# Counting every fifth group of edge tiles during the message stage of a two-layer graph network on one Trainium2 core

## The chip, the cores and the metric

The kernel runs on one core of one Trainium2 (trn2) chip. The metric is the device time in microseconds (us) of that core, as the median of several executions. The engines are TensorE (PE; its weight loads are shown apart as PEld), VectorE (DVE), ScalarE (ACT), GpSimd (POOL) and SyncE (SP, which here only issues transfers). The engines run their own instruction streams in order and meet at semaphores.

## The reference

There are N = 12,500 nodes with C = 96 features and E = 412,500 directed edges, sorted by target, with 4 features each. Cut to what matters:

```python
h = relu(layernorm(x))                       # nodes
e = mlp(edge_attr)                           # 4 -> 96, relu, batch norm over all edges
m = mlp(concat(h[src], h[dst], e))           # 288 -> 96 per edge, relu, batch norm over all edges
x = x + segment_sum(m, dst) + mlp(h)         # layer 1
h = relu(layernorm(x))
f = segment_sum((h @ W)[src] * dinv[src] * dinv[dst], dst)   # layer 2
x = x + relu(f @ W1 + b1) @ W2 + b2
```

Layer 2's sum over edges acts on 32 columns: W and W1 are multiplied together ahead, so that each node has a row t of 32 numbers, and what is wanted for each target is the sum of t over its sources.

## The kernel before, in words

The edges are cut in 806 blocks of 512 (`ES`), each of 4 tiles of 128. Nodes are padded to 12,800 = 100 columns of 128 (`HI` = 100). The stages run one after the other, with a barrier between them: set-up and node products, a pass over all edges for the statistics of the edge features (which also gathers the rows of every sixth block and keeps them in device memory), **the message stage**, the node stage between the layers, **the counting stage** of layer 2, and the output.

**The message stage** (functions at lines 918 to 1071, streams at 1243 to 1293) is software-pipelined over the 806 blocks. Every engine runs the same `step(k)`, in which some operations belong to block k and others to earlier blocks. What order each engine has in step K:

- PE: `edge_product(K)` (L983, one bf16 product of 512 columns), `message_product(K-1)` (L1017, 4 fp32 products, each shown as 2 loads and 2 products), `sum_edges(K-2)` (L1061, the same).
- DVE: `onehot_T(K)` (L998), `window_rows(K)` (L975), `onehot(K)` (L1005), `add_gathered(K-1)` (L1030), `accumulate(K-2)` (L1052), `add_window(K-2)` (L1071). The first two wait for `message_product(K-2)`, `add_gathered(K-1)` for `message_product(K-1)` and the gathered rows, `add_window(K-2)` for `sum_edges(K-2)`.
- ACT: `copy_indices(K)` (L923), `edge_relu(K-2)` (L990), `message_relu(K-3)` (L1038), `square(K-3)` (L1045).
- POOL: `gather(K)` (L932), 4 indirect transfers of 128 rows each, for 5 of 6 blocks, into one of 4 buffers. It waits until `add_gathered(K-4)` has freed the buffer.
- SP: `load_pair` (L954, L958) loads edge features and target numbers of two blocks, `load_window` (L967) the rows of the window of targets, `load_spilled` (L941) the kept rows.

**The counting stage** (from L1646) takes 3,234 tiles of 128 edges in NG = 154 groups of GT = 21. For tile n, `edge_onehots` (DVE, L1701 and L1702) makes one-hots of 600 and of 128 columns from the source (600 = 100 columns of nodes times 6 slots of targets, `SLOT` = 6), `tile_counts` (PE, L1709) multiplies them in two products of 300 columns, and `keep_counts` (ACT, L1718) copies the 600 counts to `adj` as bf16. There are three buffers between each two of these engines. When a group is complete, `group_sums` (PE, L1731) multiplies its 100 blocks of 128 x 128 counts by t, spread over the last 17 of the next group's 21 tiles; `group_parts`, `group_place` and `group_add` (L1739 to L1753) add the group's targets into the result.

Of the kernel before, what the change touches and what calls it, by code (L numbers as in the profile page):

```python
# [39 lines left out]
QS = GT * SLOT  # L40
NEG = -1e30


class Dims:


    def __init__(self, n, e):
        self.N, self.E = n, e
        self.NCH = -(-(n + W) // CH)
        self.NP = self.NCH * CH  # L50
        self.NT = self.NP // P
        self.SV = -(-e // ES)
        self.S = -(-self.SV // (2 * SPILL)) * 2 * SPILL
        self.EP = self.S * ES
        self.T = self.S * SUP
        self.NG = -(-self.SV * SUP // GT)
        self.TD = GT * self.NG

# [37 lines left out]
def gnn_kernel(nc, d, a, out):  # L96
# [4 lines left out]
    with ctx:  # L101
# [34 lines left out]
        NSPILL = SV // SPILL  # L136
        spilled = dram("spilled", (NSPILL, P, SUP * C))
# [60 lines left out]
        dstbc = x_flat[:, 2 * ES:6 * ES].bitcast(I32).rearrange("p (b s e) -> p b s e", b=2, e=ES)  # L198
# [682 lines left out]
        wraw = x_flat[:, 6 * ES:6 * ES + 2 * C].rearrange("p (b c) -> p b c", b=2)  # L881
# [14 lines left out]
        s_add = signal("s_add", 2)  # L896
        def was_spilled(k):
            return k % SPILL == SPILL - 1
# [44 lines left out]
        def load_pair(sp, i, k):  # L943
            if msgs.absent(i, k):
                return
            if k % HP:
                return
            b = (k // HP) % 2
            e0 = (MT * i + k) * ES
            sp.wait_ge(r_mm.sem, r_mm.at(MT * i + k + 1 - 4))  # L950
            sp.sem_inc(turn, 1)
            for j in range(PARTS):
                r = j * PARTS * KE
                sp.dma_start(rk[r:r + PARTS * KE, b, :, :].rearrange("p s e -> p (s e)"),  # L954
                             attr_rows[:, bass.ds(e0, HP * ES)]).then_inc(r_land[b], 16)
            sp.wait_ge(ohT_ok.sem, ohT_ok.at(MT * i + k + 1 - 4))
            sp.sem_inc(turn, 1)
            sp.dma_start(dstbc[C:P, b, :, :].rearrange("p s e -> p (s e)"),  # L958
                         a["dst_row"][:, bass.ds(e0, HP * ES)].partition_broadcast(W)).then_inc(d_land[b], 16)
# [17 lines left out]
        def edge_product(pe, i, k):  # L977
            if msgs.absent(i, k):
                return
            if k % HP == 0:  # L980
                pe.wait_ge(r_land[(k // HP) % 2], (i * (MT // 4) + k // 4 + 1) * (16 * PARTS))
            pe.wait_ge(r_ok.sem, r_ok.at(MT * i + k - 2))
            pe.matmul(ps_r(k), w36[:, :], rk[:, (k // HP) % 2, k % HP, :], start=True, stop=True).then_inc(r_mm.sem, 1)  # L983
# [8 lines left out]
        def onehot_T(dve, i, k):  # L992
            if msgs.absent(i, k):
                return
            if k % HP == 0:
                dve.wait_ge(d_land[(k // HP) % 2], (i * (MT // 4) + k // 4 + 1) * 16)
            dve.wait_ge(m_mm.sem, m_mm.at(MT * i + k - 2))
            dve.tensor_scalar(lhs[C:P, k % 2, :], dstbc[C:P, (k // HP) % 2, k % HP, :], winid[C:P, bass.ds(MT * i + k, 1)],  # L998
                              None, ALU.is_equal).then_inc(ohT_ok.sem, 1)
# [77 lines left out]


# [163 lines left out]
        with nc.If(windowed):  # L1242
            with nc.Block() as block:
                @block.gpsimd
                def _(g):
                    def step(i, k):
                        gather(g, i, k)
                    msgs.run(g, step, 0)

                @block.sync  # L1250
                def _(sp):
                    def step(i, k):
                        load_pair(sp, i, k)
                        load_window(sp, i, k)
                        load_spilled(sp, i, k)
                    msgs.run(sp, step, 0)

                @block.tensor
                def _(pe):
                    for x in (r_mm, m_mm, s_mm):  # L1260
                        x.start(pe)
                    def step(i, k):
                        edge_product(pe, i, k)
                        message_product(pe, *msgs.earlier(i, k, 1))
                        sum_edges(pe, *msgs.earlier(i, k, 2))
                    msgs.run(pe, step, 2)

                @block.scalar
                def _(act):
                    for x in (r_ok, m_ok, m_sq):  # L1270
                        x.start(act)
                    def step(i, k):
                        copy_indices(act, i, k)
                        edge_relu(act, *msgs.earlier(i, k, 2))
                        message_relu(act, *msgs.earlier(i, k, 3))
                        square(act, *msgs.earlier(i, k, 3))
                    msgs.run(act, step, 3)

                @block.vector
                def _(dve):  # L1280
                    dve.memset(sT[:, 0:NP], 0.0).then_inc(m0, 1)
                    dve.memset(acc[:, :, :], 0.0).then_inc(m0, 1)
                    dve.wait_ge(m0, 2)
                    for x in (ohT_ok, w_ok, m_pre, m_acc, s_add):
# [364 lines left out]
        HI = NT  # L1649
        KW = HI * SLOT  # L1650
        HB = KW // 2
# [15 lines left out]
        o_slot = oh[:, 0:2, :, :].rearrange("p b t w -> p b (t w)")  # L1667
        t_load = sem("t_load")
# [6 lines left out]
        a_zero = sem("a_zero")  # L1675
        e_oh = sem("e_oh")
# [6 lines left out]
        BJ = 4  # L1683
        BPER = [-(-HI * (j + 1) // (GT - BJ)) - -(-HI * j // (GT - BJ)) for j in range(GT - BJ)]

# [4 lines left out]
        def ps_b(g):  # L1690

            return bank[6][:, (g % 2) * P:(g % 2) * P + C]

        def ps_w(g):

            return bank[7][0:H, (g % 2) * P:(g % 2) * P + P]

        def edge_onehots(dve, n):
            if n >= 3:
                dve.wait_ge(a_mm, n - 2)  # L1700
            dve.tensor_scalar(o_key[:, n % 3, :], iota_k, key_f[:, n:n + 1], None, ALU.is_equal)  # L1701
            dve.tensor_scalar(o_lo[:, n % 3, :], iota_l, lo_f[:, n:n + 1], None, ALU.is_equal).then_inc(e_oh, 1)  # L1702
# [10 lines left out]
        def keep_counts(act, n):  # L1713
            g, j = n // GT, n % GT
            act.wait_ge(a_mm, n + 1)
            if j == 0 and g >= 2:
                act.wait_ge(b_mm, g - 1)
            act.activation(adj[:, g % 2, :, j * SLOT:(j + 1) * SLOT].rearrange("p (b h) s -> p b h s", b=2),  # L1718
                           ps_a(n).rearrange("p b (h s) -> p b h s", s=SLOT), ACT.Copy).then_inc(a_ok, 1)

        def group_sums(pe, g, q):

            if q == 0:
                if g == 0:
                    pe.wait_ge(a_zero, 2)
                    pe.wait_ge(t_rest, 2)
                pe.wait_ge(a_ok, GT * (g + 1))
                if g >= 1:
                    pe.wait_ge(b_sum, 2 * g)
            for h in range(sum(BPER[:q]), sum(BPER[:q + 1])):  # L1730
                ins = pe.matmul(ps_b(g), adj[:, g % 2, h, :], t3[:, h, :], start=(h == 0), stop=(h == HI - 1))  # L1731
# [3 lines left out]
        def group_parts(dve, g):  # L1735
            dve.wait_ge(b_mm, g + 1)
            if g >= 2:
                dve.wait_ge(w_mm, g - 1)
            dve.tensor_reduce(part[:, g % 2, :], ps_b(g).rearrange("p (i c) -> p c i", i=PARTS), AX, ALU.add).then_inc(b_sum, 1)  # L1739
            dve.tensor_scalar(o_slot[:, g % 2, :], iota_p[:, :], grel[:, g:g + 1], None, ALU.is_equal).then_inc(b_sum, 1)  # L1740

        def group_place(pe, g):
            pe.wait_ge(b_sum, 2 * g + 2)
            if g >= 1:
                pe.wait_ge(w_add, g)
            pe.matmul(ps_w(g), part[:, g % 2, :], o_slot[:, g % 2, :], start=True, stop=True).then_inc(w_mm, 1)

        def group_add(dve, g):
            base = dve.value_load(gbase_i[:, g:g + 1], min_val=0, max_val=N - 1)
            dve.wait_ge(w_mm, g + 1)  # L1750
            if g >= 1:
                dve.wait_ge(w_add, g)
            nodes_of = sT[0:H, bass.ds(base, P)]  # L1753
            dve.tensor_tensor(nodes_of, nodes_of, ps_w(g), ALU.add).then_inc(w_add, 1)

        with nc.If(windowed):
            with nc.Block() as block:
                @block.sync
                def _(sp):
                    sp.dma_start(t_f.rearrange("p (c k) f -> p c k f", k=CT),  # L1760
                                 t_tab.rearrange("(c p k) f -> p c k f", k=CT, p=P)).then_inc(t_load, 16)
                    sp.wait_ge(t_load, 16)

                @block.gpsimd
                def _(g):
# [3 lines left out]
                    for b in range(2):  # L1769
                        g.memset(adj[:, b, :, QS:P], 0.0).then_inc(a_zero, 1)  # L1770

                @block.tensor
                def _(pe):
# [4 lines left out]
                    for g in range(NG + 2):  # L1778
                        for j in range(GT):
                            if g < NG:  # L1780
                                tile_counts(pe, g * GT + j)
                            if 1 <= g <= NG and j >= BJ:
                                group_sums(pe, g - 1, j - BJ)
                            if g >= 2 and j == 6:
                                group_place(pe, g - 2)

                @block.scalar
                def _(act):
# [4 lines left out]
                    for n in range(TD):  # L1793
# [3 lines left out]
                def _(dve):  # L1797
# [24 lines left out]
                    for g in range(NG + 2):  # L1822
                        for j in range(GT):
                            if g < NG:
                                edge_onehots(dve, g * GT + j)
                            if g >= 2 and j == 2:
                                group_parts(dve, g - 2)
                            if g >= 2 and j == 12:
                                group_add(dve, g - 2)
# [167 lines left out]
```

## Time and profile before

| | |
|---|---|
| time, median of 3 runs | 6530.68 us (6529.23 to 6531.93) |
| time of the profiled execution | 6520.64 us |
| its span, first to last instruction | 6518.9 us |
| mean granted TensorE clock | 0.650 |
| busy: PE, PEld, DVE, ACT, POOL | 5654.6, 4382.9, 4173.9, 3822.2, 3237.0 us |
| message stage, first to last L983 | 922.9 to 4328.8 us |
| counting stage, first to last L1718 | 4627.3 to 6450.6 us |

Busy times are sums over the whole span. Those of the stages differ, so a stage has to be read by its own stretch. A busy PE is not a PE at its peak: the ends of its products are modelled, and the granted clock (0.5 is 1.2 GHz, 1.0 is 2.4 GHz) says how fast it may run.

### The profile page before, as it was taken

The page shows a single profiled execution, that of the slowest core. Times are in us where ns is not written, and L with a number is a line of the kernel's source. Part 1 is how long each engine was busy: PE and PEld are TensorE (multiplying, and loading weights), DVE is VectorE, ACT ScalarE, POOL GpSimd, SP SyncE. Part 2 cuts the span into 40 slices and gives each one's busy share as a digit, 9 for nine tenths or more (in the row PEclk, how much of TensorE's full clock was granted, in tenths as well). Part 3 has the DMA queues.
Part 4 walks back from the last instruction along what each step waited for, and adds up shares of the span by engine and source line. Part 5 has one row for each costly group of instructions (what it writes and reads, how often), then busy time and mean ns, then how long its engine had stood idle before and what let it go on. Part 6 is the DMA issues. An engine that isn't in the chain of part 4 may idle for free. (4 is left out here: it accounts for less than half of the span.)

```text
span 6518.9 us, 128731 instructions
## 1 busy us (share of the span) xinstructions
PE 5654.6 (87%) x38038; PEld 4382.9 (67%) x38038; DVE 4173.9 (64%) x13072; ACT 3822.2 (59%) x7170; POOL 3237.0 (50%) x3406
## 2 busy tenths in 40 slices
PE   6755559999999999999999999977799999999998
PEld 5311127777777777777777777765477777777777
DVE  5577764545454544445454444553799999999996
ACT  3566644434444444444444444433699999999996
POOL 3577757777777777777777777753000000000000
PEclk8555555555555555555555555555799999999998
DMA  4444433333333333333333333321000000000001
GB/s 155 137 123 124 124 83 74 74 76 75 76 75 76 74 76 74 74 76 75 75 75 76 74 75 75 74 79 30 18 2 2 2 2 2 2 2 2 2 2 62
DMA packets 297570, 400.07 MB, mean 61 GB/s; under 512 B 146679, under 2 KB 203015, under 8 KB 296247
## 3 DMA queue, kind: packets, MB, share of 16 engines
q1 hardware_dynamic: 193543, 233.00, 12.1%
q0 software_dynamic: 103344, 158.83, 11.5%
q8 instruction: 323, 5.29, 0.3%
q14 instruction: 360, 2.95, 0.1%
HBM read 333.74 MB, written 57.67 MB: 60 GB/s over the span
## 5 line engine op out<-in xcount | busy, mean ns | idle before, releaser
L932 POOL DMA_INDIRECT gbuf<-a_tab,idxb x2688 | 2580.4, 960 | 859.0 <-issue 812.3
L1718 ACT ACTIVATE nf<-psum 128x600 bf16<-128x600 f32 x3234 | 1824.2, 819 | 4.8 <-PE psum L1709 4.8
L1017 PEld LDWEIGHTS psum<-rhs,lhs 128*128 128x128 f32 x6448 | 1434.3, 327 | 365.8 <-issue 365.8
L1017 PE MATMUL psum<-rhs,lhs 128*128 128x96 f32 x6448 | 1628.7, 434 | 13.5 <-DVE rhs L975 13.5
L1038 ACT ACTIVATE msg<-pre 128x384 f32<-128x384 f32 x806 | 421.8, 523 | 1991.2 <-DVE pre L1030 1988.7
L1030 DVE TENSOR_TENSOR pre<-psum,gbuf 128x384 f32<-128x384 f32 x806 | 448.2, 556 | 1613.6 <-issue 1130.0
L1709 PE MATMUL psum<-x_all 128*128 128x300 bf16 x6468 | 1358.8, 291 | 121.6 <-DVE x_all L1702 44.6
L1061 PE MATMUL psum<-oh,msg 128*97 128x32 f32 x6448 | 1171.1, 344 | 282.4 <-ACT msg L1038 276.7
L1061 PEld LDWEIGHTS psum<-oh,msg 128*97 128x97 f32 x6448 | 1134.0, 282 | 364.1 <-ACT msg L1038 358.7
L1701 DVE TENSOR_SCALAR x_all<-x_all,dstrel 128x600 bf16<-128x600 f16 x3234 | 1193.8, 369 | 87.4 <-PE psum L1709 63.0
L1731 PE MATMUL psum<-x_all,nf 128*128 128x96 bf16 x15400 | 1074.4, 205 | 1.0 <-ACT nf L1718 1.0
L1731 PEld LDWEIGHTS psum<-x_all,nf 128*128 128x128 bf16 x15400 | 937.7, 97 | 165.9 <-issue 1.8
L1702 DVE TENSOR_SCALAR x_all<-x_all,src_i 128x128 bf16<-128x128 bf16 x3234 | 788.2, 244 | 0.0
L1709 PEld LDWEIGHTS psum<-x_all 128*128 128x128 bf16 x6468 | 421.5, 96 | 360.8 <-DVE x_all L1702 241.8
L793 PE MATMUL psum<-x_all,w 36*96 36x512 bf16 x806 | 394.4, 638 | 280.7 <-DMA x_all<-attr_parts 278.1
L836 DVE BATCH_NORM_STATS2 sT<-x_all 96x6 f32<-96x512 f32 x806 | 493.1, 676 | 181.0 <-ACT x_all L813 180.5
L744 POOL DMA_INDIRECT gbuf<-a_tab,idxb x536 | 506.0, 944 | 179.3 <-issue 150.6
L813 ACT ACTIVATE x_all<-psum,par 96x1024 f32<-96x1024 f32 x403 | 425.5, 1105 | 231.7 <-PE psum L793 229.1
L990 ACT ACTIVATE lhs<-psum,par 96x512 f32<-96x512 f32 x806 | 539.2, 669 | 3.9
L983 PE MATMUL psum<-x_all,w 36*96 36x512 bf16 x806 | 530.9, 659 | 4.5 <-DMA x_all<-attr_parts 4.4
L793 PEld LDWEIGHTS psum<-x_all,w 36*96 36x96 bf16 x806 | 118.0, 180 | 556.5 <-DMA x_all<-attr_parts 490.3
L1052 DVE TENSOR_TENSOR acc<-acc,sq 128x384 f32<-128x384 f32 x806 | 441.9, 548 | 0.6 <-ACT sq L1045 0.6
(198 smaller groups left out, 3340.3 us busy)
## 6 DMA issues: line engine op xcount, KB each, us to landing
gbuf<-a_tab,idxb POOLq DMA_INDIRECT x3224
x_all<-dst_row SPq DMA_DIRECT2D x403, 128.0 KB
x_all<-attr_parts SPq DMA_DIRECT2D x807, 36.0 KB
x_all<-attr_parts SPq DMA_DIRECT2D x1209, 24.0 KB
spilled<-gbuf SPq DMA_DIRECT2D x134, 192.0 KB, 1.9
gbuf<-spilled SPq DMA_DIRECT2D x134, 192.0 KB
x_all<-b_tab SPq DMA_DIRECT2D x806, 12.0 KB
attr_parts<-sT SPq DMA_DIRECT2D x72, 136.0 KB, 1.9
```

What stands on the lines that cost most here:

```text
L744: g.indirect_dma_start(gbuf[:, j, t, :], None, a_tab[:, :], bass.IndirectOffsetOnAxis(ap=idxb[:, j, t:t + 1], axis=0)).then_inc(x_land[j], 16)
L793: pe.matmul(bank[k % 6][0:C, :], w36[:, :], ek[:, q % NB, k % HG, :], start=True, stop=True).then_inc(e_mm.sem, 1)
L932: g.indirect_dma_start(gbuf[:, k % 4, t, :], None, a_tab[:, :], bass.IndirectOffsetOnAxis(ap=idxb[:, k % 4, t:t + 1], axis=0)).then_inc(g_ ...
L983: pe.matmul(ps_r(k), w36[:, :], rk[:, (k // HP) % 2, k % HP, :], start=True, stop=True).then_inc(r_mm.sem, 1)
L990: act.activation(lhs[0:C, k % 2, :], ps_r(k), ACT.Relu, bias=par[:, B_EDGE:B_EDGE + 1]).then_inc(r_ok.sem, 1)
L1017: ins = pe.matmul(ps_m(k)[:, t, :], lhs[:, k % 2, t * TILE:(t + 1) * TILE], rhs[:, k % 2, :], start=True, stop=True)
L1061: ins = pe.matmul(ps_s(k), msg[:, k % 2, t, :], oh[:, k % 4, t, :], start=(t == 0), stop=(t == SUP - 1))
L1701: dve.tensor_scalar(o_key[:, n % 3, :], iota_k, key_f[:, n:n + 1], None, ALU.is_equal)
L1702: dve.tensor_scalar(o_lo[:, n % 3, :], iota_l, lo_f[:, n:n + 1], None, ALU.is_equal).then_inc(e_oh, 1)
L1709: ins = pe.matmul(ps_a(n)[:, b, :], o_lo[:, n % 3, :], o_key[:, n % 3, b * HB:(b + 1) * HB], start=True, stop=True)
L1718: act.activation(adj[:, g % 2, :, j * SLOT:(j + 1) * SLOT].rearrange("p (b h) s -> p b h s", b=2), ps_a(n).rearrange("p b (h s) -> p b h s ...
L1731: ins = pe.matmul(ps_b(g), adj[:, g % 2, h, :], t3[:, h, :], start=(h == 0), stop=(h == HI - 1))
```

## The change

Of the 154 groups, 30 (numbers 4, 9, 14, ... 149) are taken out of the counting stage and counted in the message stage, one tile in each of 21 of 26 steps; the last 26 of the 806 steps have none. So 630 steps get a tile and 176 don't.

- Message stage, DVE: after `window_rows(K)` and ahead of `onehot(K)`, `early_keys` (in one of 26 steps: six small operations on 21 columns, each waiting for the one before) and `early_onehots(K)` (the one-hots of 600 and 128 columns).
- PE: `early_counts(K, 0)` between `edge_product(K)` and `message_product(K-1)`, and `early_counts(K, 1)` between that and `sum_edges(K-2)`: a bf16 product of 300 columns each. The first waits for this step's one-hots.
- ACT: after `edge_relu(K-2)`, two `early_keep` (128 x 300, to bf16), each waiting for its product, and at a group's end two transfers to device memory (`adj_tab`), each 128 x 6,300 bf16 = 1.61 MB.
- SP: the edge features of a pair of blocks come in one transfer and not in three; the target numbers come block by block, in two buffers of one block (two of two before).
- A few operations ahead of the message stage's steps (iota, two copies, two products with 315 columns, two subtractions).
- Counting stage: 124 groups of 21 tiles go through it as before; `group_sums` of a group is spread over the last 14 tiles (`BJ` = 7). The counts of the 30 early groups are loaded from device memory in four pieces, 3.23 MB a group, as soon as the products of the early group before are done, and `early_sums` multiplies their 100 blocks, spread over the 42 tiles of the windows w with w % 4 of 2 and 3.

```diff
+        self.early = [g for g in range(4, self.NG, 5)][:self.SV // EARLY]
...
-            for j in range(PARTS):
-                r = j * PARTS * KE
-                sp.dma_start(rk[r:r + PARTS * KE, b, :, :].rearrange("p s e -> p (s e)"),
-                             attr_rows[:, bass.ds(e0, HP * ES)]).then_inc(r_land[b], 16)
-            sp.wait_ge(ohT_ok.sem, ohT_ok.at(MT * i + k + 1 - 4))
+            sp.dma_start(rk[:, b, :, :].rearrange("p s e -> p (s e)"),
+                         attr_rows[:, e0:e0 + HP * ES].unsqueeze(0).to_broadcast([PARTS, PARTS * KE, HP * ES])
+                         ).then_inc(r_land[b], 16)
+
+        def load_targets(sp, i, k):
+            sp.wait_ge(ohT_ok.sem, ohT_ok.at(MT * i + k - 2))
             sp.sem_inc(turn, 1)
+            sp.dma_start(dstbc[C:P, k % 2, :],
+                         a["dst_row"][:, bass.ds((MT * i + k) * ES, ES)].partition_broadcast(W)).then_inc(d_land[k % 2], 16)
...
+        def early_tile(k):
+            g, j = k // EARLY, k % EARLY
+            return (g, j, g * GT + j) if g < NE and j < GT else None
+
+        def early_onehots(dve, k):
...
+            if n >= 2:
+                dve.wait_ge(n_mm, 2 * (n - 1))
+            dve.tensor_scalar(key_e[:, n % 2, :], iota_ke, keys[:, e % 2, j:j + 1], None, ALU.is_equal)
+            dve.tensor_scalar(low_e[:, n % 2, :], iota_le, lows[:, e % 2, j:j + 1], None, ALU.is_equal).then_inc(n_oh, 1)
+
+        def early_counts(pe, k, b):
...
+            if b == 0:
+                pe.wait_ge(n_oh, n + 1)
+            if n:
+                pe.wait_ge(n_ok, 2 * n + b - 1)
+            pe.matmul(bank[6 + b][:, 0:HB], low_e[:, n % 2, :], key_e[:, n % 2, b * HB:(b + 1) * HB],
+                      start=True, stop=True).then_inc(n_mm, 1)
+
+        def early_keep(act, k, b):
...
+            act.wait_ge(n_mm, 2 * n + b + 1)
+            if j == 0 and b == 0 and e:
+                act.wait_ge(o_adj, 32 * e)
+            act.activation(stage[:, b * HI // 2:(b + 1) * HI // 2, j * SLOT:(j + 1) * SLOT],
+                           bank[6 + b][:, 0:HB].rearrange("p (h s) -> p h s", s=SLOT), ACT.Copy).then_inc(n_ok, 1)
+
+        def early_store(act, k):
...
+            act.wait_ge(n_ok, 2 * GT * (e + 1))
+            for b in range(2):
+                act.dma_start(adj_tab[e, :, b * HI // 2 * QS:(b + 1) * HI // 2 * QS],
+                              stage[:, b * HI // 2:(b + 1) * HI // 2, :].rearrange("p h s -> p (h s)")).then_inc(o_adj, 16)
...
                     def step(i, k):
                         edge_product(pe, i, k)
+                        early_counts(pe, MT * i + k, 0)
                         message_product(pe, *msgs.earlier(i, k, 1))
+                        early_counts(pe, MT * i + k, 1)
                         sum_edges(pe, *msgs.earlier(i, k, 2))
...
                         copy_indices(act, i, k)
                         edge_relu(act, *msgs.earlier(i, k, 2))
+                        early_keep(act, MT * i + k - 2, 0)
+                        early_keep(act, MT * i + k - 2, 1)
+                        early_store(act, MT * i + k - 2)
                         message_relu(act, *msgs.earlier(i, k, 3))
...
                         onehot_T(dve, i, k)
                         window_rows(dve, i, k)
+                        early_keys(dve, MT * i + k)
+                        early_onehots(dve, MT * i + k)
                         onehot(dve, i, k)
...
-        BJ = 4
+        BJ = 7
...
+        def early_load(sp, e):
+            if e == 0:
+                sp.wait_ge(t_rest, 2)
+            else:
+                sp.wait_ge(h_mm, e)
...
-                    for g in range(NG + 2):
+                    for w in range(ND + 2):
                         for j in range(GT):
-                            if g < NG:
-                                tile_counts(pe, g * GT + j)
-                            if 1 <= g <= NG and j >= BJ:
-                                group_sums(pe, g - 1, j - BJ)
-                            if g >= 2 and j == 6:
-                                group_place(pe, g - 2)
+                            if w < ND:
+                                tile_counts(pe, w * GT + j)
+                            if w >= 2 and j == 3:
+                                group_place(pe, w - 2, False)
+                            if 1 <= w <= ND and j >= BJ:
+                                group_sums(pe, w - 1, j - BJ)
+                            if w % 4 >= 2 and w // 4 < NE:
+                                early_sums(pe, w // 4, (w % 4 - 2) * GT + j)
+                            if w % 4 == 0 and 1 <= w // 4 <= NE and j == 10:
+                                group_place(pe, w // 4 - 1, True)
...
-                    for n in range(TD):
+                    for n in range(ND * GT):
                         keep_counts(act, n)
```

## Rows read from the trace of the kernel before

**Rows 1.** The page: tenths busy in 40 slices of the span.

```profile
PE   6755559999999999999999999977799999999998
ACT  3566644434444444444444444433699999999996
POOL 3577757777777777777777777753000000000000
PEclk8555555555555555555555555555799999999998
```

**Rows 2.** Windows: length, then busy us of PE, PEld, DVE, ACT, POOL; clock, DMA.

```profile
1120.00:4300.00 3180.00, 2921.05 (x12829) 2467.63 (x12828) 1580.26 (x4524) 1294.61 (x2890) 2413.74 (x2515) 0.50 0.31 75
5000.00:5100.00 100.00, 95.38 (x1233) 73.31 (x1230) 92.99 (x381) 100.00 (x179) 0.00 (x0) 1.00 0.01 2
```

**Rows 3.** The page, costliest groups: POOL's gathers and ACT's copies of counts.

```profile
L932 POOL DMA_INDIRECT gbuf<-a_tab,idxb x2688 | 2580.4, 960 | 859.0 <-issue 812.3
L1718 ACT ACTIVATE nf<-psum 128x600 bf16<-128x600 f32 x3234 | 1824.2, 819 | 4.8 <-PE psum L1709 4.8
```

**Rows 4.** Line 983, once a step: its duration in ns, first and last start in us.

```profile
L983 PE MATMUL psum<-x_all,w x806: 631/659/660, 922.9 to 4328.8; 36*96 36x512 bf16 x162
```

**Rows 5.** Timeline of the weight loads, 2000 to 2013 us: start, length, line.

```profile
2004.12 0.15 PEld L983 LDWEIGHTS psum<-x_all,w 36*96 36x96 bf16 x1
2004.71 1.78 PEld L1017 LDWEIGHTS psum<-rhs,lhs 128*128 128x128 f32 x8 [0.44 <-issue]
2006.37 1.43 PEld L1061 LDWEIGHTS psum<-oh,msg 128*97 128x97 f32 x8
2007.86 0.15 PEld L983 LDWEIGHTS psum<-x_all,w 36*96 36x96 bf16 x1
...
2011.60 0.15 PEld L983 LDWEIGHTS psum<-x_all,w 36*96 36x96 bf16 x1
```

**Rows 6.** Timeline of VectorE in the same stretch.

```profile
2003.06 0.56 DVE L1030 TENSOR_TENSOR pre<-psum,gbuf 128x384 f32<-128x384 f32 x1 [1.11 <-PE psum L1017]
2003.54 0.55 DVE L1052 TENSOR_TENSOR acc<-acc,sq 128x384 f32<-128x384 f32 x1
2004.33 0.19 DVE L1071 TENSOR_TENSOR sT<-sT,psum 97x32 f32 x1 [0.24 <-PE psum L1061]
2004.55 0.60 DVE L998 TENSOR_SCALAR lhs<-x_all,winid 32x512 f32<-32x512 int32 x1
2005.07 0.24 DVE L975 TENSOR_TENSOR rhs<-x_all,cstb 32x96 f32<-32x96 f32 x1
2005.34 0.29 DVE L1005 TENSOR_TENSOR oh<-iota_p,dstrel 128x128 f32<-128x128 f32 x1
...
2008.91 0.49 DVE L998 TENSOR_SCALAR lhs<-x_all,winid 32x512 f32<-32x512 int32 x1
2009.33 0.25 DVE L975 TENSOR_TENSOR rhs<-x_all,cstb 32x96 f32<-32x96 f32 x1
```

**Rows 7.** Timeline of VectorE, counting stage: the one-hots of two tiles.

```profile
6202.94 0.37 DVE L1701 TENSOR_SCALAR x_all<-x_all,dstrel 128x600 bf16<-128x600 f16 x1
6203.22 0.25 DVE L1702 TENSOR_SCALAR x_all<-x_all,src_i 128x128 bf16<-128x128 bf16 x1
6203.39 0.37 DVE L1701 TENSOR_SCALAR x_all<-x_all,dstrel 128x600 bf16<-128x600 f16 x1
```

**Rows 8.** Timeline of PE, counting stage: counts and sums, two tiles.

```profile
5000.48 0.42 PE L1709 MATMUL psum<-x_all 128*128 128x300 bf16 x2
5000.74 0.37 PE L1731 MATMUL psum<-x_all,nf 128*128 128x96 bf16 x5
5001.00 0.43 PE L1709 MATMUL psum<-x_all 128*128 128x300 bf16 x2
```

**Rows 9.** Timeline of VectorE, set-up: small operations that wait for each other.

```profile
9.79 0.25 DVE L364 TENSOR_TENSOR cstb<-trep,acc 4x96 f32<-4x96 f32 x1
10.07 0.20 DVE L365 CAST acc<-cstb 4x96 bf16<-4x96 f32 x1
```

**Rows 10.** Windows at the output's loads (columns as in Rows 2), and the issue of x.

```profile
6460.00:6470.00 10.00, 7.75 (x32) 7.30 (x31) 1.89 (x8) 2.67 (x5) 0.00 (x0) 0.50 0.97 398
...
L265 SPq DMA_DIRECT2D x_all<-x x2: 419/4108/7797, 3.2 to 11.0; - x2
```

More of the change, by code:

```diff
@@ L40 @@
 QS = GT * SLOT
+EARLY = 26
 NEG = -1e30
@@ L57, in __init__ @@
         self.TD = GT * self.NG
+        self.early = [g for g in range(4, self.NG, 5)][:self.SV // EARLY]
+        self.late = [g for g in range(self.NG) if g not in self.early]
+        self.NE, self.ND = len(self.early), len(self.late)
 class Signal:
@@ L1719, in keep_counts, with group_sums @@
                            ps_a(n).rearrange("p b (h s) -> p b h s", s=SLOT), ACT.Copy).then_inc(a_ok, 1)
-        def group_sums(pe, g, q):
+        def group_sums(pe, w, q):
             if q == 0:
-                if g == 0:
+                if w == 0:
                     pe.wait_ge(a_zero, 2)
                     pe.wait_ge(t_rest, 2)
[L1727 to L1731, printed above, removed]
+                pe.wait_ge(a_ok, GT * (w + 1))
+                if w >= 1:
+                    pe.wait_ge(w_add, w)
+            for h in share(HI, GT - BJ, q):
+                ins = pe.matmul(bank[6][:, 0:C], adj[:, w % 2, h, :], t3[:, h, :], start=(h == 0), stop=(h == HI - 1))
@@ L1732, in group_sums @@
             if q == GT - BJ - 1:
                 ins.then_inc(b_mm, 1)
[L1735 to L1746, printed above, removed]
@@ new lines, in early_sums, with sums_of @@
+        def early_sums(pe, e, q):
+            if q == 0:
+                if e == 0:
+                    pe.wait_ge(h_zero, 4)
+                pe.wait_ge(h_land, 64 * (e + 1))
+                if e >= 1:
+                    pe.wait_ge(hw_add, e)
+            for h in share(HI, 2 * GT, q):
+                ins = pe.matmul(bank[7][:, 0:C], early_block(h), t3[:, h, :], start=(h == 0), stop=(h == HI - 1))
+            if q == 2 * GT - 1:
+                ins.then_inc(h_mm, 1)
+        def sums_of(early):
+            return (bank[7], 1, h_mm, h_sum, hw_mm, hw_add, d.early) if early else (bank[6], 0, b_mm, b_sum, w_mm, w_add, d.late)
@@ new lines, in group_parts, with group_place @@
+        def group_parts(dve, n, early):
+            ps, k, mm, summed, placed, added, groups = sums_of(early)
+            g = groups[n]
+            dve.wait_ge(mm, n + 1)
+            dve.tensor_reduce(part[:, k, :], ps[:, 0:C].rearrange("p (i c) -> p c i", i=PARTS), AX, ALU.add).then_inc(summed, 1)
+            dve.tensor_scalar(o_slot[:, k, :], iota_p[:, :], grel[:, g:g + 1], None, ALU.is_equal).then_inc(summed, 1)
+        def group_place(pe, n, early):
+            ps, k, mm, summed, placed, added, groups = sums_of(early)
+            pe.wait_ge(summed, 2 * n + 2)
+            pe.matmul(ps[0:H, P:2 * P], part[:, k, :], o_slot[:, k, :], start=True, stop=True).then_inc(placed, 1)
@@ L1762, in _ @@
                     sp.wait_ge(t_load, 16)
+                    for e in range(NE):
+                        early_load(sp, e)
                 @block.gpsimd
```

181 lines of the change are left out of this document (147 added, 34 removed).

## The prediction

> **What bounds the kernel now.** I read the slices of the page first, then windows by stage, then the costliest groups, then timelines of single steps. The slices show two long regimes [rows 1]. In the message stage PE is busy nine tenths at a granted clock of 0.5 (1.2 GHz), POOL seven tenths, ACT four. In the counting stage ACT is full, PE nearly, the clock is 1.0 (2.4 GHz) and POOL is idle.
>
> Counting stage: ACT is busy 100 of 100 us [rows 2], 3,234 copies in 1,824.2 us [rows 3], so 0.564 us a tile.
>
> Message stage: the 806 steps start from 922.9 to 4328.8 us [rows 4], 4.23 us a step. PE at its fastest needs 3.74: L983 starts at 2004.12 and 2007.86, and again 3.74 later at 2011.60 [rows 5]. The rest is POOL's: 2,688 gathers cost 2580.4 busy and 812.3 idle "issue" us [rows 3], 1.26 us each; 4 gathers in 5 of 6 steps make 4.21 us a step. So the stage runs at POOL's pace, with 0.49 us a step of slack on PE.
>
> **The step with a tile.** The sum of added work isn't what counts here; the order is. Write K for a step with a tile. DVE ends its step K-1 with `add_window(K-3)`, which waits for `sum_edges(K-3)`, the last thing in PE's step K-1. Only then come `onehot_T(K)`, `window_rows(K)` and the new one-hots. PE, after `edge_product(K)`, now waits for those one-hots ahead of `message_product(K-1)`; before, that product needed only DVE's step K-1. So PE and DVE take turns: a ring from the end of PE's step through half of DVE's and back, once a step. Along it, from the start of L983(K):
>
> - `add_window` starts at +0.21 (2004.12 to 2004.33), L998 at +0.43 [rows 5, 6]. L975 follows L998 by 0.42 in one step and 0.52 in the other, L1005 follows L975 by 0.27 [rows 6]. In L1005's place stands the new one-hot, at +1.12 to +1.22.
> - The second one-hot starts 0.28 later and takes 0.25 [rows 7]: ready at +1.65 to +1.75. I take 1.70.
> - `early_counts(K, 0)`: no row has this product at 1.2 GHz. L983 is the nearest: 0.15 load, then 0.44 until the next load starts, 0.59 for 512 columns [rows 5]. 512 columns at 1.2 GHz are 0.43, 300 are 0.25; with the load 0.40. Bounds 0.25 (load hidden) and 0.41. Then `message_product` starts at +2.10 where it started at +0.59: **+1.51**.
> - `early_counts(K, 1)`: again 0.40, bounds 0.25 and 0.41 (L983 behind L1061 pays the load in full [rows 5]).
>
> Together 3.74 + 1.51 + 0.40 = **5.65 us** a step with a tile, with the lower ends 5.30, with the upper 5.72. The new waits for ACT are off this ring: `early_keep` stands behind `edge_relu`, and ACT is idle over half the stage [rows 2]. Queued behind `early_keep(K, 1)` is `message_relu(K-1)`, which needs DVE's addition behind `message_product(K-1)` and so could hardly start earlier. POOL, at 4.21, is now ahead of everybody: its four buffers are full when a step without a tile comes.
>
> **The message stage.** 630 steps at 5.65 are 3,560. The 150 steps without a tile between groups run from full buffers at PE's 3.74: 561. The last 26 stay at 4.23: 110. `early_keys`: 6 linked operations at 0.28 [rows 9], 1.7 us in the ring, 30 times: 50. The lead-in: 3. Sum 4,284 before transfers.
>
> The stores: 3.23 MB a group onto queues that carried 75 GB/s at a share of 0.31 [rows 2]. At 398 GB/s [rows 10] a group is 8 us of all engines, in the 5 steps without a tile, when loads and gathers have least slack. ACT may also be held at its second issue (a second large one took SP 7.8 us, the first 0.42 [rows 10]); 2 to 3 us of that pass unseen, since the message it delays is multiplied a step later. Bounds 0 and 10 us a group; I take 1.5, since buffers are full then: 45. SP's load of target numbers is issued two steps ahead, 7.5 us at the least, and it has two transfers less to issue per pair: nothing; without that cover it would be a wait in the ring.
>
> Stage: 4,329. Before: 806 x 4.23 = 3,409. **+920** (with the ends of the step, +700 to +960; with those of the stores, -45 and +255 more).
>
> **The counting stage.** 630 copies less: 630 x 0.564 = **-355**. PE per tile: two counts and five or six sums take 0.52 [rows 8]; the two counts 0.26 (5000.48 to 5000.74), and the 5.9 sums of a tile (100 over 17) the other 0.26, 0.044 each. In the 60 windows that also carry early sums, a window's PE work is 21 x 0.26 + 150 x 0.044 = 12.1 and some 0.3 for placing; ACT's is 21 x 0.564 = 11.8. In its last 14 tiles PE needs 0.26 + 9.5 x 0.044 = 0.68 a tile, in the first 7 0.36, and three buffers carry only two tiles across. So 0.5 us a window is lost: **+30** (bounds 0 and 100). DVE's one-hots run at 0.45 a tile alone [rows 7], below 0.564. The early loads have two windows, 23.7 us, for 3.23 MB: 136 GB/s against 398 seen [rows 10], hidden; without that cover each would hold PE, 30 times.
>
> **Sum.** 920 - 355 + 30 = +595. The profiled execution took 6520.6, the median of the runs 6530.7, 10 us above. So 6520.6 + 595 = 7116 on its scale and 7,125 as a median.
>
> **A rule against one term.** The row: behind L983 the next load starts only after 0.44 us of idle PEld, when the product's columns have gone through [rows 5], so I charged loads in full. The Trainium skill (TensorE: Matmul & The Clock Gate, Part 2: What happens when you issue a matmul) says that PE pulls the next weight load ahead of running products, into a background buffer. By that rule both early products would cost their columns alone. What this would make is the second rival below.
>
> **The rivals.**
>
> 1. The ring doesn't close: the one-hots arrive in time, and only PE's work counts. Then 26 steps cost PE 21 x 4.54 + 5 x 3.74 = 114 us against POOL's 110: +4 in 30 rounds, 120; with 50 and 45 for keys and stores and -325 for counting, 6,420. With products at 0.25, 6,300. For it: DVE is busy only half the stage [rows 2]. Against: the chain `sum_edges`, `add_window`, one-hots, product is in program order on both engines, and in rows 6 the wait of L1071 for PE shows. This is the case in which the change is faster. Chance 0.07.
> 2. The ring closes with hidden loads: 630 x 0.30 = 189 less, 6,935. Chance 0.12.
> 3. Stores disturb the stage: the steps without a tile wait out 8 to 10 us a group, or ACT's held issue delays sums by several us: +240 more, 7,370. Chance 0.10.
> 4. PE takes over as the bound of the whole counting stage, or waits for early loads: 5 us a window lost in the 60 is +300; a third of that is likelier, 7,220. Chance 0.08.
> 5. The clock rises to 2.4 GHz in the message stage, since bf16 products are added. For it: the counting stage, with such products, has 1.0 [rows 2]. Against: it is 0.50 over the whole stretch [rows 2], steps in which PE never pauses [rows 5] among them, and in the ring PE stands still a fifth of the time. PE's part of the ring would halve, the ring would fall to 3.7 and POOL bind again: -325 and some 95, 6,300. Chance 0.03.
>
> **How the numbers follow.** The forecast, steps of about 5.65 us and the counting stage down by 325, has 0.60. The range runs from the second rival to the third: with the ends of the terms 6,890 to 7,400. Faster by over 0.2% (about what a measurement of this kernel can tell from no change) are rivals 1 and 5, 0.10; within 0.2% only an accident of both, 0.01; slower 0.89.
>
> **What the changed profile would show.** L983 first to last some 900 us further apart; steps of 5.6 to 5.7 us in runs of 21, then five of 3.7; before the early product PE idle over 1 us, ended by the second early one-hot on DVE; POOL idle for `add_gathered`. The clock 0.5. The counting stage with 2,604 copies in about 1,500 us, ACT full but for two windows in four. I'm wrong if steps with a tile take 4.6 us or less, or if PE's wait ahead of the early product is absent.

## The result: 6907.9 us against 6530.8, 5.8% slower

The changed kernel took 6907.89 us (6905.49 to 6908.81), the kernel before 6530.79 (6529.23 to 6531.93); the ratio is 1.0577 (95% interval 1.0559 to 1.0595). Forecast were 7,125 us and a range of 6,890 to 7,400. The profiled execution took 6907.84 us, its span is 6905.1.

The page of the changed kernel, tenths busy in 40 slices, and the groups that answer to [rows 1, 3]:

```profile
PE   7655558888888888888888888888967999999998
ACT  3566634444444444444444444444424999999996
...
POOL 3677756666666666666666666666631000000000
PEclk7555555555555555555555555555556999999998
...
L970 POOL DMA_INDIRECT gbuf<-a_tab,idxb x2688 | 2587.1, 962 | 1506.8 <-issue 896.5
L1861 ACT ACTIVATE nf<-psum 128x600 bf16<-128x600 f32 x2604 | 1521.9, 760 | 11.2 <-PE psum L1852 4.8
...
L1164 PEld LDWEIGHTS psum<-x_all 128*128 128x128 bf16 x1260 | 194.3, 154 | 1058.7 <-DVE x_all L1153 1058.7
```

In the message stage TensorE went from nine tenths to eight and GpSimd from seven to six, though there is more to do, and no engine is fuller than TensorE's eight: the sign of a wait, not of a new full engine. GpSimd's idle time before its gathers went from 859 to 1507 us, so it no longer sets the pace. The last line names the wait: 1058.7 us of idle weight loading ahead of the early product (L1164), ended by the second early one-hot (L1153). The clock stayed at 0.5.

The stage's length is read from L1024, the edge product (L983 before), that of the counting stage from L1861 (L1718 before), the first and the last start:

```profile
L1024 PEld LDWEIGHTS psum<-x_all,w x806: 148/152/153, 937.3 to 5010.5; 36*96 36x96 bf16 x162
...
L1861 ACT ACTIVATE nf<-psum x2604: 652/716/1092, 5309.3 to 6836.5; 128x600 bf16<-128x600 f32 x186
```

Message stage: 4073.2 us, against 4328.8 - 922.9 = 3405.9 [rows 4]: +667. Counting stage: 1527.2 us against 1823.3: -296. The rest of the span's +386 is the start: L983 ran twice ahead of a 10.7 us clearing before; L1024 first runs behind it, 14 us later.

One counted step of the changed kernel, weight loads and then VectorE (start, length), which answers to [rows 5, 6]:

```profile
3003.80 0.15 PEld L1024 LDWEIGHTS psum<-x_all,w 36*96 36x96 bf16 x1
3005.62 0.10 PEld L1164 LDWEIGHTS psum<-x_all 128*128 128x128 bf16 x1 [1.66 <-DVE x_all L1153]
3005.80 1.78 PEld L1057 LDWEIGHTS psum<-rhs,lhs 128*128 128x128 f32 x8
3007.40 0.20 PEld L1164 LDWEIGHTS psum<-x_all 128*128 128x128 bf16 x1
3007.62 1.52 PEld L1101 LDWEIGHTS psum<-oh,msg 128*97 128x97 f32 x8
3009.20 0.15 PEld L1024 LDWEIGHTS psum<-x_all,w 36*96 36x96 bf16 x1
```

```profile
3004.01 0.19 DVE L1111 TENSOR_TENSOR sT<-sT,psum 97x32 f32 x1 [0.52 <-PE psum L1101]
3004.23 0.60 DVE L1038 TENSOR_SCALAR lhs<-x_all,winid 32x512 f32<-32x512 int32 x1
3004.75 0.24 DVE L1016 TENSOR_TENSOR rhs<-x_all,cstb 32x96 f32<-32x96 f32 x1
3005.03 0.38 DVE L1152 TENSOR_SCALAR x_all<-x_all,rstd 128x600 bf16<-128x600 f16 x1
3005.32 0.25 DVE L1153 TENSOR_SCALAR x_all<-x_all,mean 128x128 bf16<-128x128 bf16 x1
```

The ring can be read off by going back and forth: TensorE's last product ends, VectorE adds the window (4.01), makes the message's one-hot and window rows, the early one-hots (5.03, 5.32), and TensorE's early load starts at 5.62, 0.05 us after the second has ended. Between its edge product and that load the loader stands idle 1.66 us; 0.44 us of this stood there before the change as well [rows 5]. The step takes 9.20 - 3.80 = 5.40 us. Most steps take 5.29 or 5.39, by whether L1038 takes 0.48 or 0.60: 5.34 in the mean.

### The profile page after: what moved, and what is told of

The parts are those of the page before. It is cut to its first block and busy times, and to the rows that moved or that the text cites. A ratio compares the mean times of both kernels' runs of the same rounds, so it can differ in the third digit from the quotient of the medians.

```text
span 6905.1 us, 129865 instructions
## 1 busy us (share of the span) xinstructions
PE 5617.6 (81%) x38042; PEld 4418.8 (64%) x38042; DVE 4287.1 (62%) x13256; ACT 4072.6 (59%) x7800; POOL 3245.4 (47%) x3411
## 5 line engine op out<-in xcount | busy, mean ns | idle before, releaser
L1057 PE MATMUL psum<-rhs,lhs 128*128 128x96 f32 x6448 | 1600.5, 430 | 0.0
L1861 ACT ACTIVATE nf<-psum 128x600 bf16<-128x600 f32 x2604 | 1521.9, 760 | 11.2 <-PE psum L1852 4.8
L1057 PEld LDWEIGHTS psum<-rhs,lhs 128*128 128x128 f32 x6448 | 1435.1, 327 | 126.2 <-issue 78.0
L1175 ACT ACTIVATE x_all<-psum 128x300 bf16<-128x300 f32 x1260 | 534.0, 424 | 1586.3 <-PE psum L1164 1586.2
L1101 PEld LDWEIGHTS psum<-oh,msg 128*97 128x97 f32 x6448 | 1206.3, 285 | 14.8 <-ACT msg L1078 8.9
L1164 PE MATMUL psum<-x_all 128*128 128x300 bf16 x1260 | 561.2, 446 | 740.9 <-DVE x_all L1153 740.9
L1101 PE MATMUL psum<-oh,msg 128*97 128x32 f32 x6448 | 1132.0, 338 | 7.6 <-ACT msg L1078 7.6
L1852 PE MATMUL psum<-x_all 128*128 128x300 bf16 x5208 | 1071.6, 291 | 76.2 <-DVE x_all L1845 30.6
L1844 DVE TENSOR_SCALAR x_all<-x_all,dstrel 128x600 bf16<-128x600 f16 x2604 | 966.6, 371 | 101.0 <-PE psum L1852 11.0
L1164 PEld LDWEIGHTS psum<-x_all 128*128 128x128 bf16 x1260 | 194.3, 154 | 1058.7 <-DVE x_all L1153 1058.7
L1874 PE MATMUL psum<-x_all,nf 128*128 128x96 bf16 x12400 | 804.8, 205 | 0.6 <-DVE sT L1934 0.6
L1874 PEld LDWEIGHTS psum<-x_all,nf 128*128 128x128 bf16 x12400 | 715.3, 97 | 108.6 <-ACT nf L1861 0.8
L1845 DVE TENSOR_SCALAR x_all<-x_all,src_i 128x128 bf16<-128x128 bf16 x2604 | 640.0, 246 | 0.0
L1024 PE MATMUL psum<-x_all,w 36*96 36x512 bf16 x806 | 531.1, 659 | 16.6 <-DVE x_all L1417 12.6
```

The costliest lines, as they stand in the source:

```text
L1057: ins = pe.matmul(ps_m(k)[:, t, :], lhs[:, k % 2, t * TILE:(t + 1) * TILE], rhs[:, k % 2, :], start=True, stop=True)
L1101: ins = pe.matmul(ps_s(k), msg[:, k % 2, t, :], oh[:, k % 4, t, :], start=(t == 0), stop=(t == SUP - 1))
L1164: pe.matmul(bank[6 + b][:, 0:HB], low_e[:, n % 2, :], key_e[:, n % 2, b * HB:(b + 1) * HB], start=True, stop=True).then_inc(n_mm, 1)
L1175: act.activation(stage[:, b * HI // 2:(b + 1) * HI // 2, j * SLOT:(j + 1) * SLOT], bank[6 + b][:, 0:HB].rearrange("p (h s) -> p h s", s=SL ...
L1844: dve.tensor_scalar(o_key[:, n % 3, :], iota_k, key_f[:, col:col + 1], None, ALU.is_equal)
L1845: dve.tensor_scalar(o_lo[:, n % 3, :], iota_l, lo_f[:, col:col + 1], None, ALU.is_equal).then_inc(e_oh, 1)
```

## The experiments

The theory: the message stage grew because `early_counts(K, 0)` waits for one-hots that VectorE can't begin before TensorE has ended its step before. The rivals: it is the added work wherever it stands; it is the stores. A second question came from the trace: why the early products cost 0.43 us a step where the forecast had 0.80.

Experiments e1 to e4 ran on a chip on which the kernel before itself took 7747.96 us (7735.55 to 7770.36). It has no trace of its own there. The nearest is that of e4, which is the kernel before but for wider weights: its counting stage was as long as ever (1824.2 us), its message stage took 4426.5 us instead of 3406, and its engines stood for times that the profile puts down to no one ("issue", "remote"). So those four tell by ratios and by steps without a pause, and e1 to e3 were run again, on chips with the usual time. e1, e5, e6, e11 and e12 were timed 4 to 10 times; e2 to e4 and e7 to e10 once, so they tell by their traces and by differences well above the spread of one kernel's runs (6518 to 6529 us in 13 runs of the kernel before, beside e9).

**e1 and e5: the early tiles one step later.** All the work is kept; TensorE multiplies in step K the one-hots that VectorE made in step K-1.

```diff
-                        early_counts(pe, MT * i + k, 0)
+                        early_counts(pe, MT * i + k - 1, 0)
                         message_product(pe, *msgs.earlier(i, k, 1))
-                        early_counts(pe, MT * i + k, 1)
+                        early_counts(pe, MT * i + k - 1, 1)
...
-                        early_keep(act, MT * i + k - 2, 0)
-                        early_keep(act, MT * i + k - 2, 1)
-                        early_store(act, MT * i + k - 2)
+                        early_keep(act, MT * i + k - 3, 0)
+                        early_keep(act, MT * i + k - 3, 1)
+                        early_store(act, MT * i + k - 3)
```

> TensorE and ScalarE take each early tile one step later (early_counts of block K-1 in step K, early_keep likewise), with all the work kept. Ring theory (TensorE waits in every counted step for one-hots that VectorE can only start once TensorE's step before has ended): the wait of about 1.0 us is gone, a counted step costs TensorE 3.74 + 0.43 = 4.17 us, below GpSimd's 4.21 a step, so the message stage falls from 4073 to about 3430 us and the time from 6908 to about 6270 us, faster than the kernel before. Rival, it is the added work: the order of the steps changes nothing, 6908 us. Rival, the stores to device memory: their part stays, some 6300 to 6400 us, with the waits in the five steps without a tile.

Measured: 7594.64 us, 0.9791 (0.9760 to 0.9822) of the kernel before. The sign turned, against the kernel before on the same chip; a step without a pause took 4.05 us.

> The same kernel as e1_later (early tiles taken one step later by TensorE and ScalarE), beside a kernel before that takes its usual 6530 us. On the first chip steps without a pause took TensorE 4.05 us instead of 5.3, below GpSimd's 4.21 a step. Ring theory: about 6270 us. If it is the added work whatever the order: 6908 us. If the stores hold the five steps without a tile: 6300 to 6400 us.

Measured: 6246.27 us (6244.77 to 6250.02) against 6522.91, ratio 0.9578 (0.9564 to 0.9593). The trace of e5: weight loads of one step, then, for the stretch from 1120 to 4300 us, the longest waits of GpSimd and of the addition of the gathered rows (total us, times, longest).

```profile
3000.79 0.15 PEld L1024 LDWEIGHTS psum<-x_all,w 36*96 36x96 bf16 x1
3001.38 0.11 PEld L1164 LDWEIGHTS psum<-x_all 128*128 128x128 bf16 x1 [0.44 <-issue]
3001.38 1.84 PEld L1057 LDWEIGHTS psum<-rhs,lhs 128*128 128x128 f32 x8
3003.05 0.20 PEld L1164 LDWEIGHTS psum<-x_all 128*128 128x128 bf16 x1
3003.26 1.52 PEld L1101 LDWEIGHTS psum<-oh,msg 128*97 128x97 f32 x8
3004.84 0.15 PEld L1024 LDWEIGHTS psum<-x_all,w 36*96 36x96 bf16 x1
```

```profile
DVE pre L1070 <- issue: 772.5, 308, 8.1
POOL gbuf L970 <- issue: 759.5, 2491, 0.3
```

Of the idle 1.66 us the 0.44 behind L1024 are left, and the step is 4.05 us. The stage's first and last L1024 start at 935.0 and 4349.2: 3414 us, 8 more than before the change, with all 630 tiles in it. GpSimd sets the pace again, back to back with 0.3 us between gathers; the additions wait up to 8.1 us. (The profile names no releaser for them; that it is the gathered rows is read from the program's order.) The added work costs TensorE 4.05 - 3.74 = 0.31 us in such a step, which stays under GpSimd's 4.21. So neither the added work (it is all there) nor the stores made the +667: the order did.

**e2 and e9: the early one-hots first in VectorE's step; e3 and e10: behind `onehot(K)`.** If a ring exists, its length follows the place of its members. (With the early one-hots go the early keys.)

```diff
+                        early_keys(dve, MT * i + k)
+                        early_onehots(dve, MT * i + k)
                         onehot_T(dve, i, k)
                         window_rows(dve, i, k)
-                        early_keys(dve, MT * i + k)
-                        early_onehots(dve, MT * i + k)
                         onehot(dve, i, k)
```

> On VectorE the early one-hots stand first in the step, ahead of onehot_T and window_rows, with the same work. Ring theory: the ring is shorter by these two, 0.41 + 0.41 us or a little less, so a counted step falls from 5.3 to 5.4 us to about 4.6 us, the time from 6908 to about 6440 us. Rival, it is the added work: no change, 6908 us.

> On VectorE the early one-hots stand behind onehot(K), with the same work. Ring theory: the ring is longer by that operation, 0.28 us, so a counted step takes about 5.6 us and the time is 6908 + 630 x 0.28 = about 7085 us. Rival, it is the added work: no change, 6908 us.

On the first chip, one run each: 7887.37 and 8002.80 us; steps without a pause of 4.48 and 5.49 us, where the changed kernel has 5.34.

> The same kernel as e2_first (early one-hots first in VectorE's step), beside a kernel before that takes its usual 6520 to 6530 us. On the first chip the counted step without a pause fell from 5.34 to 4.48 us. Ring theory: 630 x 0.86 = 540 us less than the changed kernel, about 6370 us; TensorE's step is then 0.3 us above GpSimd's 4.21. Rival, added work: 6908 us.

> The same kernel as e3_last (early one-hots behind onehot), beside a kernel before that takes its usual 6520 to 6530 us. On the first chip the counted step rose from 5.34 to 5.49 us. Ring theory: 630 x 0.15 = 95 us more, about 7000 us. Rival, added work: 6908 us.

Measured, one run each: 6417.53 us with the one-hots first, 7018.60 with them last; the changed kernel lies between at 6908. One step of e9 in its weight loads, one of e10:

```profile
3002.50 0.15 PEld L1024 LDWEIGHTS psum<-x_all,w 36*96 36x96 bf16 x1
3003.58 0.10 PEld L1164 LDWEIGHTS psum<-x_all 128*128 128x128 bf16 x1 [0.93 <-DVE x_all L1153]
...
3007.16 0.15 PEld L1024 LDWEIGHTS psum<-x_all,w 36*96 36x96 bf16 x1
```

```profile
3000.49 0.15 PEld L1024 LDWEIGHTS psum<-x_all,w 36*96 36x96 bf16 x1
3002.41 0.11 PEld L1164 LDWEIGHTS psum<-x_all 128*128 128x128 bf16 x1 [1.76 <-DVE x_all L1153]
...
3005.98 0.15 PEld L1024 LDWEIGHTS psum<-x_all,w 36*96 36x96 bf16 x1
```

Same instructions, three orders. The rows of e9 and of the changed kernel show the longer of their two common steps, that of e10 the shorter; by the median over the 630 early loads TensorE's wait ahead of them is 0.75, 1.57 and 1.76 us. e9 is 490 us faster, of 540 expected: its steps are 4.48 or 4.66 us. e10 adds 111 us, of 95 expected; from the place alone e3 had expected 0.28 us a step and found 0.15 in the first run and 0.19 in the mean here (5.53 against 5.34), part of it because L1038 is in its slow form of about 0.60 us in 42 of 600 steps instead of 227.

**e12: the early keys off the ring.** The six small operations move to the last of the five steps without a tile (those of the first group stay in step 0).

```diff
-            if k >= SV or k % EARLY or k // EARLY >= NE:
+            if k and (k % EARLY != EARLY - 1 or (k + 1) // EARLY >= NE):
                 return
-            e = k // EARLY
+            e = (k + 1) // EARLY
```

> The changed kernel with early_keys one step earlier, in the last of the five steps without a tile, so that its six operations are off the ring. Ring theory: the first counted step of each group falls from 6.8 us to 5.3 to 5.4, 30 x 1.45 = 43 us, to about 6865 us. Rival, the same work stays on VectorE, no change: 6908 us.

Measured: 6865.24 us (6862.09 to 6866.54), 43 us less than the changed kernel; the first counted step of a group takes 5.38 us instead of 6.80. The same operations at the same engine cost nothing when they stand off the ring.

**e11: the new transfers alone.** The kernel before, with one transfer of edge features for three and the target numbers block by block.

```diff
-            for j in range(PARTS):
-                r = j * PARTS * KE
-                sp.dma_start(rk[r:r + PARTS * KE, b, :, :].rearrange("p s e -> p (s e)"),
-                             attr_rows[:, bass.ds(e0, HP * ES)]).then_inc(r_land[b], 16)
+            sp.dma_start(rk[:, b, :, :].rearrange("p s e -> p (s e)"),
+                         attr_rows[:, e0:e0 + HP * ES].unsqueeze(0).to_broadcast([PARTS, PARTS * KE, HP * ES])
+                         ).then_inc(r_land[b], 16)
...
+            sp.wait_ge(ohT_ok.sem, ohT_ok.at(MT * i + k - 2))
+            sp.dma_start(dstbc[C:P, k % 2, 0, :],
+                         a["dst_row"][:, bass.ds((MT * i + k) * ES, ES)].partition_broadcast(W)).then_inc(d_land[k % 2], 16)
```

> The kernel before with the change's transfers of edge features (one for three) and target numbers (one block at a time) alone. My sum had nothing for them: same time as before within 0.2%. Rival, the target numbers, now with half the buffer, come late: up to 0.3 us in each of 806 steps, 6770 us.

Measured: 6514.29 us against 6525.81, ratio 0.9983 (0.9973 to 0.9993). The halved buffer costs nothing; the kernel is even 0.2% faster with it.

**e6 and e7: the counting stage.** In the last 14 tiles of a window with early sums TensorE took longer than ScalarE. The changed kernel's PE timeline there:

```profile
5600.27 0.42 PE L1852 MATMUL psum<-x_all 128*128 128x300 bf16 x2
5600.53 0.46 PE L1874 MATMUL psum<-x_all,nf 128*128 128x96 bf16 x7
5600.83 0.25 PE L1904 MATMUL psum<-x_all,lhs 128*128 128x96 bf16 x2
5600.91 0.42 PE L1852 MATMUL psum<-x_all 128*128 128x300 bf16 x2
```

From count to count 0.64 us (0.68 with a third early sum), where ScalarE needs 0.564. The edit puts the early sums where no late sums stand: in the first 7 tiles of three windows in four.

```diff
-            for h in share(HI, 2 * GT, q):
+            for h in share(HI, 3 * BJ, q):
...
-                            if w % 4 >= 2 and w // 4 < NE:
-                                early_sums(pe, w // 4, (w % 4 - 2) * GT + j)
+                            if w % 4 >= 1 and j < BJ and w // 4 < NE:
+                                early_sums(pe, w // 4, (w % 4 - 1) * BJ + j)
```

> e5 and, in the counting stage, the early groups' sums only in the first 7 tiles of three windows in four, where no late sums stand, instead of all 42 tiles of two windows. TensorE's work per tile is then nowhere over ScalarE's 0.564 us. Theory that the counting stage loses 58 us to windows in which TensorE has 0.66 us of work a tile: e5 minus about 58, so about 6210 us. Rival, the loss there is from placing and adding groups: no change against e5. Rival, the early loads now land too late (19.7 us for what took 9): some windows stall, slower than e5.

> The changed kernel with the spread of e6 alone. If the two losses are independent: 6908 - 58 = about 6850 us, with the message stage as it was (4073 us) and every window of the counting stage at 11.85 us.

Measured: e6 6191.18 us (6186.28 to 6195.14), ratio to before 0.9490 (0.9477 to 0.9503), 55 less than e5; e7 6848.22 us (one run), 60 less than the changed kernel. The counting stage of e6 and of e7, from its copies' first and last start, and 200 us of the changed kernel and of e6 (columns as in [rows 2]):

```profile
L1861 ACT ACTIVATE nf<-psum x2604: 652/826/1090, 4652.8 to 6124.0; 128x600 bf16<-128x600 f32 x186
```

```profile
L1861 ACT ACTIVATE nf<-psum x2604: 653/821/1087, 5305.7 to 6776.5; 128x600 bf16<-128x600 f32 x186
```

```profile
5400.00:5600.00 200.00, 194.44 (x2760) 153.47 (x2758) 183.21 (x740) 199.15 (x341) 0.00 (x0) 1.00 0.18 67
```

```profile
4800.00:5000.00 200.00, 197.20 (x2865) 160.50 (x2864) 191.10 (x773) 200.00 (x355) 0.00 (x0) 1.00 0.18 67
```

1471 us in both, 56 less than 1527, and 355 copies in 200 us instead of 341. ScalarE looks full in either, at 199 and 200: a copy that waits a little for its product hardly shows as idle time, so the count of copies is the thing to read. The two losses are independent: the spread gives 55 us with the ring opened and 60 us with it closed. e6 is the fastest version of this study, 5.1% faster than the kernel before.

**e4 and e8: what the edge product does to the load behind it.** In the kernel before, 0.44 us of idle loader stand behind L983 [rows 5]. Is it its width or its rows?

```diff
 e4
-        w36 = sb("w36", [KR, C], BF16)
+        w36 = sb("w36", [KR, P], BF16)
...
-            pe.matmul(ps_r(k), w36[:, :], rk[:, (k // HP) % 2, k % HP, :], start=True, stop=True).then_inc(r_mm.sem, 1)
+            pe.matmul(bank[k % 2][:, :], w36[:, :], rk[:, (k // HP) % 2, k % HP, :], start=True, stop=True).then_inc(r_mm.sem, 1)
 e8
-        w36 = sb("w36", [KR, C], BF16)
+        w36 = sb("w36", [P, C], BF16)
...
-            pe.matmul(ps_r(k), w36[:, :], rk[:, (k // HP) % 2, k % HP, :], start=True, stop=True).then_inc(r_mm.sem, 1)
+            pe.matmul(ps_r(k), w36[:, :], rk_all[:, (k // HP) % 2, k % HP, :], start=True, stop=True).then_inc(r_mm.sem, 1)
```

> The kernel before, with the edge product's weights widened from 96 to 128 columns (zeros in the last 32), to see why 0.44 us of idle weight loading stands behind that product (L983) while only 0.18 us stands between the early product's load and the next. If the width of the weights decides: the gap of 0.44 falls to under 0.1 us and the back-to-back step from 3.74 to about 3.4 us. If the 36 rows, or the 512 columns that stream, decide: the gap stays and the step is 3.74 us. The time stays near 6520 us in both cases, since GpSimd sets the step.

> The kernel before, with the edge product padded from 36 to 128 rows (zeros), 96 columns of weights as before. If the 36 rows decide that the next weight load waits out the product (the gap of 0.44 us, which 128 columns of weights left as it was): the gap falls under 0.25 us and the back-to-back step from 3.74 to about 3.4 us. If it is the kind of the load behind it (fp32 behind bf16): the gap stays 0.44. Total near 6520 us in both cases.

One run each. Weight loads of e4, then of e8:

```profile
3006.95 0.10 PEld L984 LDWEIGHTS psum<-x_all,w 36*128 36x128 bf16 x1
3007.49 1.78 PEld L1018 LDWEIGHTS psum<-rhs,lhs 128*128 128x128 f32 x8 [0.44 <-issue]
```

```profile
3009.85 0.20 PEld L986 LDWEIGHTS psum<-x_all,w 128*96 128x96 bf16 x1
3009.93 2.04 PEld L1020 LDWEIGHTS psum<-rhs,lhs 128*128 128x128 f32 x8
3011.85 1.43 PEld L1064 LDWEIGHTS psum<-oh,msg 128*97 128x97 f32 x8
```

With 128 columns of weights the load is shorter (0.10 against 0.15) and the gap stays. With 128 rows the gap is gone: the next load starts 0.08 us after the start of the edge product's own. L1064 then starts 2.00 us after the edge product's load instead of 2.25, and the shortest steps of the trace are 3.31 us instead of 3.74. The time is unmoved (e4 7737.05 against 7747.96, e8 6517.52 against 6522.91), since GpSimd sets the step. The kind of the load behind it doesn't decide either: in e5's trace the early product's load, bf16 and of 128 rows, also starts only 0.44 us after L1024's load has ended. So it was the product's 36 rows.

## Why the prediction was right, and where its terms were off

Right were the direction, the mechanism and the place: the ring, with the one-hots ready at +1.66 or +1.76 (forecast +1.65 to +1.75), the plain steps at 3.74, GpSimd no longer the bound, the clock at 0.5, the new transfers and ScalarE's waits at nothing (TensorE's waits ahead of the early products are all put down to VectorE's one-hots). Each of these is either in a row above or moved by an experiment. The figure that had the chance of 0.60, steps of about 5.65 us, did not come. The time came 217 us under the forecast, inside the range, for these terms:

- **The early products**, 0.40 each in the sum, cost 0.18 and 0.25 (5.62 to 5.80; and L1057 to the next L1024 in 3.40 us, where L1017 to L983 took 3.15). That is 0.37 a step; 0.05 of it is used up between the end of the one-hot and the load. The counted step is 5.34 us instead of 5.65: 630 x 0.31 = **-195**. This is the term that was mis-sized, at the step "L983 is the nearest", and with it the choice to charge the loads in full. The row was read rightly and was the wrong row. Its 0.44 us belongs to a product of 36 rows (e8); behind a product of all 128 rows, as the early ones are, the next load starts 0.18 us after the early load has started, before 300 columns at 1.2 GHz (0.25 us) can have gone through. The rule of the Trainium skill that was weighed there (TensorE: Matmul & The Clock Gate, Part 2: What happens when you issue a matmul) held for the early products, and the exception was the row. What happened is the forecast's second rival, given a chance of 0.12 and the time 6,935; it took 6,908. That the rival's time is met so closely is in part luck: the terms below add up to only -22, with single ones of -39 and +28.
- **The stores**, 45 in the sum: in the 30 groups the third step without a tile takes 3.93 us in the mean instead of 3.74, all others 3.74. That is 6 us and **-39**, if that step is all they cost; no run left them out. ScalarE took 0.40 us for an issue in the median and 1.80 at most; the second issue was not held as that of the much fuller start was [rows 10].
- **The keys**, 50: the first counted step takes 6.80 instead of 5.34, 44 us, and e12 gave 43 back: **-6**.
- **The last 26 steps**, 110: up to the last start they are 25 steps and took 100, 4.0 us each instead of 4.23: **-10**.
- **Before the change** the stage was 3,409 by the sum and 3,406 in the rows: **+3**. The start moved by 14 us rather than 3, since L983's head start was lost: **+11**.
- **The counting stage**, +30 of losses in the sum, lost 1527 - 2604 x 0.564 = 58: **+28**. The work per tile was foreseen (0.68), but I let three buffers carry two tiles across each window. A window with early sums took 12.95 us in the mean against 11.84 before, so 1.1 us were lost instead of 0.5, and the second window behind each pair of them was 0.25 us shorter than usual. That the buffers carried less than two tiles is worked out from this; no run changed their number. e6 and e7 give the loss back by spreading the sums.
- **From span to median**: I added 10 us, as the profiled execution before was that much faster than the median; the profiled one of the changed kernel is at its median: **-9**.

What stays open: why L1038 takes about 0.60 us instead of 0.48 in some steps of the ring. Over the 600 counted steps that are not the first of their group it was so in 227. In each of these a gather's record on GpSimd ends 0.33 to 0.43 us after L1038 has started, and in none of the other 373 does one end 0.3 to 0.6 us after it. The two go together; which causes which was not tested. And why the first chip, that of e1 to e4, took longer for every kernel was not explained.

## What to carry to other kernels

In a software pipeline the place of a step counts more than its length: before work is put into a wait-free slot of one engine, follow what its producer waits for, one step back, and see whether the path returns to the same engine. Here the early products made TensorE's step 1.60 us longer in place (3.74 to 5.34) and 0.31 us one step later (4.05), which GpSimd's pace hid. When a new operation has no row of its own, ask of the nearest row what is peculiar to it (here the 36 rows) before taking its gap over.

## What the runs showed that was not expected

- Behind a product of 36 rows the next weight load waited out its 512 columns (0.44 us at 1.2 GHz); padded with zeros to 128 rows, in another buffer, that load started 0.08 us after the start of the product's own load and a back-to-back step fell from 3.74 to 3.31 us.
- bf16 weights of 36 rows and 128 columns loaded in 0.10 us, those of 36 rows and 96 columns in 0.15 (e4 against the kernel before, both at 1.2 GHz).
- One chip ran the kernel before in 7748 us instead of 6531. Its traces (e1 to e4) show counting stages of the usual length and message stages in which engines stood idle with nothing in the profile to release them, in e1 for up to 18.6 us at a time (ScalarE ahead of an early copy).
